# A decoder layer on one core: attention and expert stages of two programs become one, two row slots in each turn of the attention

## The reference, cut to what matters

```python
x = layernorm(x + attn(x))              # x is (4, 512, 512): 2048 tokens of 512 numbers
x = layernorm(x + experts(x, tokens, ctx, ctx, ctx))
x = layernorm(x + (einsum('btd,rde->bte', x, factors) / sqrt(8) + bias))

def attn(h):
    i = bitlinear(h, Wi); f = sigmoid(bitlinear(h, Wf)); g = bitlinear(h, Wg)
    i = silu(i) * (1 - f)
    h = scan over the tokens of a batch: h[t] = f[t] * h[t-1] + i[t]
    return bitlinear(rmsnorm(g) * g_norm_weight * silu(h), Wo)
# bitlinear: activations rounded to 8 bits per token, weights to -1, 0, 1
def experts(h):                         # one of four experts per token, by its token id
    return (silu(h @ W[e].T) * (h @ W[e].T)) @ W[e].T      # the same 512x512 matrix three times
```

## Time and profile before

| | |
|---|---|
| median of three runs | 392.49 us (392.0, 396.09, 392.49) |
| span of the profiled execution | 391.8 us |
| the profiled execution's own time | not listed apart from its span |
| TensorE busy | 307.0 us (78%), granted clock 0.945 on average |
| VectorE busy | 260.9 us (67%) |
| ScalarE busy | 199.4 us (51%) |
| GpSimd busy | 184.8 us (47%) |
| moved by transfers | 36.10 MB |

### The profile page before, as it was taken

The page is one execution under the profiler, slowest core; times in us unless marked ns, Lnnn a source line. Parts: engine busy times, 40 slices in busy tenths (PEclk is TensorE's granted clock), DMA queues, the critical chain, the costliest instruction groups (busy, mean ns, idle before and its releaser), DMA issues.

```text
span 391.8 us, 6465 instructions
## 1 busy us (share of the span) xinstructions
PE 307.0 (78%) x1531; PEld 220.0 (56%) x1541; DVE 260.9 (67%) x654; ACT 199.4 (51%) x359; POOL 184.8 (47%) x297
## 2 busy tenths in 40 slices
PE   1165867486777769837788999999999999999870
PEld 0124344243434334415557888888888888888650
DVE  4899897488979786822545666666666666665641
ACT  3776977385666767313334444444444444444330
POOL 0338875575655574621123344444444444443342
PEclk9999899988969898995999999999999999999986
DMA  7995377657272643113001111111111111100000
GB/s 243 383 386 209 66 150 141 96 148 186 53 185 43 172 72 90 54 56 108 0 2 46 22 58 52 59 32 54 54 54 54 59 53 65 60 31 28 28 28 6
DMA packets 17735, 36.10 MB, mean 92 GB/s; under 512 B 2286, under 2 KB 2542, under 8 KB 17712
## 3 DMA queue, kind: packets, MB, share of 16 engines
q0 software_dynamic: 7056, 16.53, 17.7%
q1 hardware_dynamic: 10656, 19.31, 14.4%
HBM read 26.64 MB, written 11.02 MB: 96 GB/s over the span
## 4 chain that ended last, share of the span: by engine, by line
PE 46%; DVE 2%; issue 2%; ACT 2%; POOL 2%; DVEq 0%; POOLq 0%
PE bank L1209 13%; PE bank L1213 13%; PE bank L1210 12%; PE bank L1201 6%; PE bank L1224 2%; POOL d L1035 1%; DVE st L1126 1%; ACT rows L1104 0%; ACT x L1099 0%; DVE mv L1132 0%; POOL v L1033 0%; POOL out L1049 0%; DVE b L1137 0%; DVE r L1163 0%; ACT x L1092 0%
## 5 line engine op out<-in xcount | busy, mean ns | idle before, releaser
L1033 POOL TENSOR_TENSOR v<-mv,eps_c 128x1 f32<-128x1 f32 x57 | 11.6, 203 | 112.7 <-DVE mv L1132 112.4
L873 PE MATMUL bank<-w_q,xq_t 128*128 128x512 bf16 x191 | 52.2, 434 | 6.0 <-issue 5.3
L1144 DVE TENSOR_TENSOR hid<-bank,act_z 128x512 f32<-128x512 f32 x19 | 13.1, 691 | 42.8 <-ACT act_z L1081 42.8
L873 PEld LDWEIGHTS bank<-w_q,xq_t 128*128 128x128 bf16 x192 | 21.0, 112 | 34.6 <-issue 17.0
L1074 ACT ACTIVATE h_hi<-bank 128x512 fp32r<-128x512 f32 x19 | 11.4, 599 | 46.2 <-PE bank L1201 46.2
L1035 POOL TENSOR_TENSOR d<-v,minus_half 128x1 f32<-128x1 f32 x57 | 32.4, 568 | 4.5
L1209 PE MATMUL bank<-f_hi,m_hi 128*128 128x512 f32 x76 | 32.0, 421 | 0.7 <-ACT m_hi L1074 0.7
L1092 ACT ACTIVATE x<-r,b,d 128x512 f32<-128x512 f32 x19 | 15.5, 816 | 32.4 <-DVE b L1137 32.4
L1209 PE MATMUL bank<-c_hi,h_hi 128*128 x76 | 31.5, 415 | 0.3 <-issue 0.2
L1209 PE MATMUL bank<-c_hi,a_hi 128*128 x76 | 30.2, 397 | 1.0 <-ACT a_hi L1074 0.8
L1210 PE MATMUL bank<-f_lo,m_hi 128*128 128x512 f32 x76 | 30.7, 404 | 0.0
(11 more groups left out here) (155 smaller groups left out, 832.7 us busy)
## 6 DMA issues: line engine op xcount, KB each, us to landing
f_sum<-in_factors POOLq DMA_DIRECT2D x7, 1024.0 KB, 9.3
rows<-sorted_rows SPq DMA_DIRECT2D x19, 256.5 KB, 2.6
c_stage<-in_ctx_t SPq DMA_DIRECT2D x8, 512.0 KB, 6.2
xs<-in_x SPq DMA_DIRECT2D x1, 3072.0 KB, 18.9
w_stage<-in_wi_t SPq DMA_DIRECT2D x1, 1024.0 KB, 5.9
xs<-in_x SPq DMA_DIRECT2D x2, 512.0 KB, 8.8
w_stage<-in_wf_t SPq DMA_DIRECT2D x1, 1024.0 KB, 8.4
w_stage<-in_wg_t SPq DMA_DIRECT2D x1, 1024.0 KB, 10.5
```

The lines of the kernel that those rows point to most:

```text
L873: last = t.matmul(bank[:], xq_t[:, j, c, :], w_q[:, m, c, :], start=(c == 0), stop=(c == KC - 1))
```

## The change

One `nc.Block()` holds all the work, and every loop is written out.

- **Slots.** A slot is numbered in the order in which it fills, so that slot n is complete once group (n+3)//2 is scattered (`scattered_group`); `load_rows(n)` waits for that group. The last slots wait for all groups.
- **Turns.** A short part before turn 1 does group 0. Turns 1 to 3 do attention only (front of g, back of g-1). Turns 4 to 8 do the same (turn 8 has no front) and the work of two slots each: "down" of slot n-1, "up" and "down" of n, "up" of n+1, "mix" of n-3 and n-2, with n = 2*turn-7. So turn 4 has four products and turns 5 to 8 have six. A tail does what is left: eight "up", nine "down", eleven "mix".
- **Attention in channel-major form.** The weights of i and f are the stationary operand, so that the products come out with channels on the partitions (32 matmuls of 256 columns in place of 16 of 512), and the 16 float32 transposes per group (L889) go. The scale per token is spread over the partitions (`spread_max`, `max_row`) and multiplied in by DVE (`rescale`, four per group). The scan reads both operands from SBUF.
- **Norms.** bn_stats and bn_aggr go. The residual's DVE instruction also sums the row (accum_out), ACT squares with the mean as bias, POOL does the rest (`power_1`, `power_2`, `power_3`). The first layernorm is done before the scatter.
- **Small chains.** The scales of x, g and o, which DVE computed for the most part, are now chains of small instructions on POOL, each waiting for the one before (`scale_x` 7, `scale_g` 6, `scale_o` 11 instructions).
- **Preparation.** All of c_hi and c_lo is done before turn 3: c_lo chunks 0 to 5 before turn 1, 6 to 11 in turn 1, 12 to 15 in turn 2. The factors are added in pairs: 1 and 2 in turn 1, 3 and 4 in turn 2, 5 and 6 in turn 3, 7 after it. ACT's `high_of_factors` stands between turns 3 and 4.

The core of the difference:

```diff
-        attention(nc, k, sem, sb, x.rearrange("b (n p) d -> p (b n) d", p=P), tok, ctx_t,
-                  (wi_t, wf_t, wg_t, wo_t), g_weight, factors, bias, ident_in, before_in, number_in, slot_in,
-                  sorted_rows)
-        experts(nc, k, sem, sb, sorted_rows, out.rearrange("b s d -> (b s) d"))
...
-                def add_factor(g):
-                    if not isinstance(g, int) or g < RANK - 1:
-                        if isinstance(g, int) and g == 0:
-                            pool.wait_ge(s.factor0, 16)
-                        else:
-                            pool.wait_ge(k.s_facc, 16 * g)
-                        hold()
-                        pool.dma_start(k.f_sum[:], factors[bass.ds((g + 1) * D, D), :].rearrange("(k p) n -> p k n", p=P),
-                                       accum_op=ALU.add).then_inc(k.s_facc, 16)
...
-        def over_batches(eng, turn):
-            for g in range(HALVES):
-                turn(g, 0, g % HALVES, lambda d: 0 <= g + d)
-            with eng.Fori(1, B - 1) as b:
-                for half in range(HALVES):
-                    turn(HALVES * b + half, b, half, lambda d: True)
-            for g in range(N_GROUPS - HALVES, N_GROUPS + 1):
-                turn(g, g // HALVES, g % HALVES, lambda d: g + d < N_GROUPS)
...
+MERGE = 3
+LEAD = 2 * MERGE + 1
+TAIL = 2 * N_GROUPS - LEAD + 2
...
+def scattered_group(n):
+
+    return min((n + 3) // 2, N_GROUPS - 1) if n < SURE else N_GROUPS - 1
...
+                def load_rows(n):
+                    after(sp, s.sq2, n - RING + 1)
+                    after(sp, s.token, n - RING + 1)
+                    for j in range(GT):
+                        sp.wait_ge(s_scat[j], 16 * (scattered_group(n) + 1))
+                    sp.dma_start(rows[:, n % RING, :], sorted_rows[n * P:(n + 1) * P, :]).then_inc(s_rows[n % RING], 16)
...
+                def add_factor(i):
+                    if i == 1:
+                        pool.wait_ge(s.factor0, 16)
+                    else:
+                        pool.wait_ge(s.facc, 16 * (i - 1))
+                    pool.dma_start(f_sum[:], chunked(factors[i * D:(i + 1) * D, :]), accum_op=ALU.add
+                                   ).then_inc(s.facc, 16)
...
+                for turn in range(1, MERGE + 1):
+                    g, p = turn, turn - 1
+                    if p >= 1:
+                        power_1(p - 1)
+                        scatter_rows(p - 1)
+                    if turn == 1:
+                        pool.wait_ge(s.padded, 16)
+                        pool.wait_ge(s.numbers_in, 16)
+                        pool.wait_ge(s.place, 1)
+                        low_of_ctx(range(6, 8))
+                    scale_o(p)
+                    quantise_o(p)
+                    number_rows(p)
+                    scale_g(g)
+                    scale_x(g + 2)
+                    if turn == 1:
+                        add_factor(1)
+                        add_factor(2)
+                        low_of_ctx(range(8, 12))
+                    if turn == 2:
+                        low_of_ctx(range(12, 16))
+                        add_factor(3)
+                        add_factor(4)
+                    if turn == 3:
+                        add_factor(5)
+                        add_factor(6)
+                token_of_row(0)
+                add_factor(7)
+                power_1(MERGE - 1)
+                scatter_rows(MERGE - 1)
+                for turn in range(MERGE + 1, N_GROUPS + 1):
+                    g, p, n = turn, turn - 1, 2 * turn - LEAD
+                    scale_o(p)
+                    quantise_o(p)
+                    power_2(n - 1)
+                    token_of_row(n)
+                    if is_group(g):
+                        scale_g(g)
+                    if n >= 2:
+                        add_bias(n - 2)
+                    if n >= 3:
+                        power_3(n - 3)
+                        store(n - 3)
+                    number_rows(p)
+                    if n >= 2:
+                        power_3(n - 2)
+                    token_of_row(n + 1)
+                    power_1(p)
+                    if n >= 2:
+                        store(n - 2)
+                    add_bias(n - 1)
+                    power_2(n)
+                    scatter_rows(p)
+                    if is_group(g + 2):
+                        scale_x(g + 2)
...
+                def high_of_factors():
+                    act.wait_ge(s.facc, 16 * (RANK - 1))
+                    for c in range(KC):
+                        a.activation(f_hi[:, c, :], f_sum[:, c, :], ACT.Copy).then_inc(s.fhi, 1)
...
+                    if p >= 1:
+                        square_1(p - 1)
+                    tanh_f(g, 0)
+                    tanh_f(g, 1)
+                    if p >= 1:
+                        norm_1(p - 1)
+                    forget(g, 0)
+                    square_o(p, 0)
+                    square_o(p, 1)
+                    silu_i(g, 0)
+                    silu_i(g, 1)
+                    forget(g, 1)
+                    square_g(g, 0)
+                    square_g(g, 1)
+                    max_row(g + 1)
+                    x_by_channel(g + 1)
+                    if turn == MERGE:
+                        high_a(0)
+                    square_x(g + 2, 0)
+                    o_by_channel(p)
+                    silu_h(g, 0)
+                    square_x(g + 2, 1)
+                    silu_h(g, 1)
+                    if turn == 1:
+                        high_of_ctx(2, range(KC))
+                        high_of_ctx(3, range(KC))
+                square_1(MERGE - 1)
+                high_of_factors()
...
+                for turn in range(MERGE + 1, N_GROUPS + 1):
+                    g, p, n = turn, turn - 1, 2 * turn - LEAD
+                    silu_h_by_token(p)
+                    if is_group(g):
+                        project_f(g)
+                    transpose_h(n - 1)
+                    if is_group(g):
+                        project_i(g)
+                    if n == 1:
+                        pe.wait_ge(s.o, GT * MERGE)
+                    down(n - 1)
+                    transpose_a(n)
+                    if is_group(g):
+                        project_g(g)
+                    if is_group(g + 1):
+                        pe.wait_ge(s.oqt, p)
+                        after(pe, s.tml, n - 2)
+                        transpose_x(g + 1)
+                        spread_max(g + 1)
+                    if n >= 3:
+                        mix(n - 3)
+                    if n >= 2:
+                        pe.wait_ge(s.xqt, min(g + 2, N_GROUPS))
+                        transpose_m(n - 2)
+                    up(n)
+                    pe.wait_ge(s.xqt, min(g + 2, N_GROUPS))
+                    after(pe, s.tml, n - 1)
+                    transpose_o(p)
+                    if n >= 2:
+                        mix(n - 2)
+                    transpose_h(n)
+                    project_back(p)
+                    transpose_a(n + 1)
+                    down(n)
+                    pe.wait_ge(s.oqt, p + 1)
+                    transpose_m(n - 1)
+                    up(n + 1)
...
-                        v.tensor_tensor_scan(h_ch[:, half, c, a, :], f_ch[:, c, a, :], b_ti[c][:, a * GW:(a + 1) * GW],
-                                             0.0 if half == 0 else h_ch[:, half - 1, c, a, GW - 1:GW],
-                                             ALU.mult, ALU.subtract).then_inc(s.scan, 1)
...
+                        v.tensor_tensor_scan(h_ch[:, c, i, :], f_ch[:, c, i, :], i_ch[:, c, i, :],
+                                             0.0 if g % 2 == 0 else h_ch[:, c, i, GW - 1:GW], ALU.mult, ALU.subtract
+                                             ).then_inc(s.scan, 1)
...
-                    v.bn_stats(st[:], r).then_inc(s_bn, 1)
...
-                    v.bn_aggr(mv[:], st[:]).then_inc(s_ag, 1)
...
+                def residual_2(n):
+                    i = slice(n % 2, n % 2 + 1)
+                    dve.wait_ge(s.y, n + 1)
+                    after(dve, s.sq3, n - RING + 1)
+                    v.scalar_tensor_tensor(x2[:, n % RING, :], bank_y[:], 1.0, rows[:, n % RING, 0:D], ALU.mult, ALU.add,
+                                           accum_out=n2_sum[:, i]).then_inc(s.r2, 1)
+                    dve.wait_ge(s.r2, n + 1)
+                    after(dve, s.b2, n - 1)
+                    v.tensor_scalar(n2_mean[:, i], n2_sum[:, i], -1.0 / D, None, ALU.mult).then_inc(s.mean2, 1)
```

1868 lines of the change are left out of this document (953 added, 915 removed).

## The result

| | before | after |
|---|---|---|
| median of the runs shown first | 392.49 us (3 runs) | 443.66 us (442.01 to 444.07, 4 runs) |
| median in the comparison | 392.61 us (392.0 to 396.09) | 443.66 us |
| span of the profiled execution | 391.8 us | 441.6 us |
| TensorE clock granted, mean | 0.945 | 0.845 |

What follows compares the result with a forecast made beforehand. VectorE was taken to bound the attention, TensorE the expert stage, and POOL's factor waits to reach the bounding engine almost whole. Before turn 4, 168; turns 27 + 96 + 27; tail 116: 434 us, range 396 to 456.

Steps and rivals of the forecast that it cites:

- The prediction's own figure for no waits at all: Whole kernel, inside the first rival: if the five factor landings cost nothing, 434 - 5 x 8.4 = 392 us.
- addition 1 issued: Start: POOL's queue, full from about 37 us, holds 28.7 us of work, so the first factor addition is issued at 66.
- last landing to slot 1: Before turn 4: from the landing at 162.9, factor sum, norms, scatters and rows' load let slot 1 be transposed at 176.0.
- turn from slot 1 to slot 3: Turn 4, the first with attention and expert work merged: 27 us, as it has no "mix".
- three turns: The full merged turns between turn 4 and turn 8: 32 us each, bounds 28.2 and 36, together 96 us.
- last turn and tail: End: turn 8 at 27 us, nothing covering its hidden layer; then 116 of tail, with slot 11 delayed by 5.
- so ACT has the first c_hi chunks at about 37 as well, and c_lo can begin: Start: the new start does much the same work as before, so POOL's c_lo begins at about 37 us.
- GpSimd and VectorE get in each other's way: Rival, chance 0.08: scans and gates reading SBUF exclude POOL, 4.3 us a turn, 30 in all: 464 us, range 452 to 470.
- The boundary chain: Across merged turns: down, residual, square, power, scatters, landing and rows' load take 30.5 us; the turn was taken as 32.
- If merged turns are near 28, TensorE is their bound and my boundary chain is not: Sign for the merged turns, forecast at about 32 us; TensorE's own work was put at 28.2 us.
- The waits cost less than I say: Rival, chance 0.10: additions land sooner or queues have more play, so five landings shrink; range 392 to 412 us.
- POOL is not on the path at all: Rival, chance 0.12: the first three turns run at VectorE's 17 us, turn 4 counts from 103: 369 us.

Runs made afterwards that it cites:

- e1: The changed kernel with all seven factor additions and their waits left out (output lacks seven factors): 393.63 us, ratio 1.003.
- e3: The changed kernel with all seven additions kept but spread over the turns, and ACT's rounded factor sum moved into turn 4: 401.35 us, ratio 1.023.
- e5: e3 with POOL issuing the scatter before store and bias, behind power_2, in turns 4 to 8: 400.83 us, ratio 1.023.
- e7: e3 with both edits, those of e5 and e6: 394.49 us, ratio 1.006.
- e9: e8 with norm_1 straight after the group's squares, the scatter before power_2, and norm_2 moved into the next turn: 392.46 us, ratio 1.000.
- e6: e3 with all 16 chunks of c_lo computed by VectorE in place of POOL: 397.08 us, ratio 1.014.
- e8: e7 with addition 1 after scale_x(2), addition 7 in mid-turn 4, and slot 0's transposes behind those of the output: 392.64 us, ratio 1.004.
- e10: e9 without any factor addition (output lacks seven factors): 378.13 us, ratio 0.964.
- e11: e9 with additions 3 to 6 each more than a landing apart, and the rounded sum and its rest in turn 5: 387.13 us, ratio 0.984.
- e12: e11 with norm_2 of slot n-1 moved on ACT behind the copy of the transposed output: 385.49 us, ratio 0.980.
- e2: The changed kernel with only ACT's rounded factor sum and VectorE's rest of it moved to the end of turn 4: 435.54 us, ratio 1.112.
- e4: The changed kernel with POOL's scatter right after power_1 and ACT's norm_1 earlier, in turns 4 to 8: 457.46 us, ratio 1.165.

## Why the prediction held, and where it was off

**The waits, right.** "POOL idle before the second and later factor additions, released by the transfer, some 8 us each, four times" was to be seen, and was: 9.26, 7.79, 9.59 and 8.08. ACT's f_hi was to wait until about 163 and waited until 171.0; the granted clock before it was 0.50 to 0.96 in windows of 10 us from 50 us on. e1 and e3 show the cause by leaving the additions out and by moving them: 393.6 and 401.4 against 443.7. The prediction's own figure for no waits at all, with the additions kept, was 392. The run that fits this is e3, 9 us above; that e1 came to 393.6 is partly luck, since it lacks the issues and transfers too.

**The sum, term by term** (span: 434 from the sum, 441.6 measured, 7.6 off):

| step | predicted | measured | off by |
|---|---|---|---|
| addition 1 issued | 66 | 69.5 | +3.5 |
| to addition 2 | 9.4 | 10.8 | +1.4 |
| to addition 3 | 30.2 | 30.3 | +0.1 |
| to addition 4 | 9.4 | 9.2 | -0.2 |
| to addition 5 | 19.7 | 21.6 | +1.9 |
| to 6, to 7, to the last landing | 28.2 | 29.6 | +1.4 |
| last landing to slot 1 | 13.1 | 11.9 | -1.2 |
| turn from slot 1 to slot 3 | 27 | 29.8 | +2.8 |
| three turns | 96 | 93.3 | -2.7 |
| last turn and tail | 135 | 135.6 | +0.6 |

Before slot 1 lie 6.9 of the 7.6 us. In the row from the last landing to slot 1 the prediction's step from 167.6 to 176.0 holds 8.4 us, where its own terms (2.7, 3.6 and 2.6) come to 8.9; the trace has 7.7. The rest of the distance to the median (443.66) is that the median lies 2.1 above the profiled span, where the prediction named 0.7 and added none. Part of the agreement is luck: the first merged turn was 2.8 us too short in the sum and the three after it 2.7 too long. The tail is not: TensorE stood 5.64 us for slot 11's rows where 5 were put, and the slots follow each other at 9.67 us, where 9.66 were.

**The start, mis-sized.** The step "so ACT has the first c_hi chunks at about 37 as well, and c_lo can begin" left out `places` on POOL, 14 small instructions from 30.5 to 39.4 us, ahead of c_lo. And `scale_o` was put at 4.0 us and took 6.3. These are 2.4 and 2.3 us; the eight chunks of c_lo gave 1.4 back (10.1 us instead of 11.5). POOL's timeline in turn 2, and again in turn 4, shows small instructions of two lengths:

```profile
92.14 0.58 POOL L287 TENSOR_TENSOR o_t<-o_ss,g_f 128x2 f32<-128x2 f32 x1
...
95.28 0.69 POOL L291 TENSOR_TENSOR o_fr<-g_f,o_r 128x2 f32<-128x2 f32 x1
96.04 0.20 POOL L293 TENSOR_TENSOR o_mf<-o_max,o_fr 128x2 f32<-128x2 f32 x1
...
177.68 0.20 POOL L287 TENSOR_TENSOR o_t<-o_ss,g_f 128x2 f32<-128x2 f32 x1
```

VectorE's timeline beside the first of them:

```profile
92.75 1.27 DVE L836 TENSOR_TENSOR_SCAN h_ch<-f_ch,i_ch 128x256 f32<-128x256 f32 x2
...
94.70 1.27 DVE L836 TENSOR_TENSOR_SCAN h_ch<-f_ch,i_ch 128x256 f32<-128x256 f32 x2
95.89 0.67 DVE L843 TENSOR_TENSOR o_tok<-bank_a,gw_b 128x512 f32<-128x512 f32 x1
```

The same instruction (L287) takes 0.58 us at 92.1 and 0.20 at 177.7. L291 still takes 0.69 beside VectorE's scans, whose operands are both in SBUF, and L293 behind it 0.20, as VectorE has come to a PSUM bank (95.89). This is the rival "GpSimd and VectorE get in each other's way": the trace bears its mechanism out, its price was wrong. It was put at 4.3 us a turn on the path. In turn 2 it is 2 us of POOL's chain (6.3, against 4.4 for the same instructions in turn 4 without their wait). The merged turns have it too: in turns 5 and 6 the quantisation beside the scans takes 2.06 and 2.29 us instead of 1.37 and the first two scans together 2.04 instead of 1.27, but these turns came out at 31 and not at 36. The Trainium skill ("GPSIMD Engine Reference", Specifications) says that GpSimd shares its SBUF interfaces with VectorE, with contention when a VectorE instruction has two SBUF inputs; the trace agrees, with 0.58 to 0.69 us beside gate and scan and 0.20 once VectorE reads a PSUM bank.

**The pairs.** A landing was costed at 9.3 to 9.4 us, the median. Between the two of a pair lie 10.8, 9.2, 11.0 and 9.6 us, so that they cost 3 more in all. What lengthened two of them no run tells.

**The merged turns.** The first was put at 27 for having no "mix" and took 29.8: TensorE stood 3.98 us in it before 193.17, for the hidden layer, and its granted clock was 0.50 in the window from 192 to 196, neither of which the sum has. The next were put at 32 and took 31.1 on average.

The boundary chain is half right. The prediction starts it at the end of "down" of slot n; in the profile (256 to 275 us) it comes over the group's residual (258.10), and goes on over power_1, store and bias. "Down" ended at about 262.1 and its square at 263.9, but its power began only at 265.83, behind the bias: it was not what POOL waited for. From the end of "down" to the transposes the sum has 13.1 us and the trace 13.1, so the number came out although the waits are others.

"If merged turns are near 28, TensorE is their bound and my boundary chain is not": the turns were near 31, but TensorE's own work is 29.1 and not 28.2, and at most 0.9 us of a turn was lost in waiting for the rows. That cutting the chain brought little (e5 and e7: 3.0 and 4.4 us by slot 11, over five turns; e9: nothing) fits this: TensorE's work and POOL's chain in the middle of the turn are hardly shorter.

**The rivals.** "The waits cost less than I say" is refuted by the trace. "POOL is not on the path at all" (369) is refuted even without additions: e1 stands at 393.6 and not at 369. Its slot 1 is transposed at 133.7, where that rival has 111 (turn 4 counting from 103), so 22.7 of the 24.6 us lie before it. TensorE's work fell from 307.0 to 288.8 us and VectorE's from 260.9 to 214.1, and the first three turns used up that gain. POOL's load is a part of the reason: e1's windows have it busy 7.6 to 8.9 of 10 us from 50 to 110, though only 5.6 and 4.7 in the two after them, and c_lo on VectorE brought slot 1 forward by 5.9 us (e6). The rest of the distance to 111 no run explains; without additions and without c_lo on POOL, and with the moves of e8, slot 1 still comes at 121.6 (e10). Of the kernels with all additions only e11 and e12, which have all these moves and the sum in turn 5, pass the old program, by 6 and 8 us beside their own runs of it.

**What stays open.** e10 says that 14 us of additions were left in e9 (spans 376.1 and 390.6); e11 and e12, at 385.8 and 383.4, have recovered 5 and 7 of them. How much of the rest is the sum and its rest in turn 5, and how much the issues and the transfers beside others, no run separates.

## What to carry to other kernels

A transfer that must wait for its predecessor belongs at least one landing behind it in the queue, with useful work between, and away from any short transfer that somebody waits for: the seven additions cost 50 us in pairs and 8 when spread (e1 to e3). The Trainium skill ("DMA: Bandwidth & Descriptors", Rules for kernel authors) asks for early issue and a late wait, and e3 gives that rule its size here, 42 us. Before moving work to an engine with free time, add up its queue in the stretch where it will be, and after each repair look for the next wait: e2, e5, e6, e8, e9 and e12 each brought less than the wait or chain that they shortened had shown, and e4 made a longer one.
